# A metaformer block on one Trainium2 core: first x tile loaded by partition halves, W1's centring moved behind the router scores, first up-projection from copied weights

## The reference

```python
x = x + _L0_conv_ref(_ln_c(x), Wqkv, bqkv, Wout, bout, 8)       # _ln_c: norm over the 64 channels
t = _to_tokens(x)                                               # (8, 1024, 64)
t = t + _L0_ffn_ref(_ln_t(t), Wr, br, W1, b1, W2, b2, gamma, beta)
...
# attention:  qkv = Wqkv @ x + bqkv; attn = softmax(q k^T) per head, 8 x 8 over the channels;
#             out = Wout @ (attn @ v) + bout
# ffn:        logits = mean over tokens(x) @ Wr + br; softmax; capacity scale; softmax; top 2; softmax
#             h = gelu(x @ W1[e] + b1[e]);  y = h @ W2[e] + b2[e];  out = sum of w_e * y over the two experts
#             return layer_norm(out + x, gamma, beta)
```

## Time and profile before

| | |
|---|---|
| median of 3 runs | 97.44 us (97.40 to 97.64) |
| the profiled execution | 97.48 us |
| its span, first to last instruction | 95.7 us |
| mean granted clock of TensorE | 0.988 of full |
| busy: PE / DVE / ACT / POOL | 83.5 / 63.5 / 50.8 / 34.6 us |
| read from and written to HBM | 5.49 MB, 2.10 MB |

### The profile page before, as it was taken

How to read it: one execution, slowest core, us unless ns; L and a number is a source line. 1 busy time by engine, 2 the same in 40 slices (tenths; PEclk the granted TensorE clock), 3 DMA queues, 4 the chain that set the end, 5 groups by cost and what they waited for, 6 DMA issues and landing times.

```text
span 95.7 us, 2267 instructions
## 1 busy us (share of the span) xinstructions
PE 83.5 (87%) x765; PEld 45.0 (47%) x765; DVE 63.5 (66%) x223; ACT 50.8 (53%) x90; POOL 34.6 (36%) x83
## 2 busy tenths in 40 slices
PE   4993999999799999969749999999989999998800
PEld 1343696899664256649613327323333332335400
DVE  0089999992649799897998886326354464659350
ACT  0000474755487412406636999995997779643000
POOL 6000000003600000005434499949272660499900
PEclk9999999999999999999999999999999999999995
DMA  2899999950000000001430015686000026018654
GB/s 48 259 405 293 301 262 295 334 110 0 0 0 7 0 0 0 3 7 31 106 82 0 10 36 137 160 191 145 0 0 0 0 70 149 7 25 194 191 138 110
DMA packets 6554, 9.82 MB, mean 103 GB/s; under 512 B 1040, under 2 KB 3344, under 8 KB 6544
## 3 DMA queue, kind: packets, MB, share of 16 engines
q1 hardware_dynamic: 4688, 6.51, 26.2%
q10 hardware_dynamic: 1856, 3.18, 11.1%
HBM read 5.49 MB, written 2.10 MB: 79 GB/s over the span
## 4 chain that ended last, share of the span: by engine, by line
PE 43%; POOL 17%; DMA 10%; DVE 8%; ACT 7%; issue 6%; POOLq 4%; ACTq 1%; SPq 1%; DVEq 0%
DMA cst<-consts_dram 7%; POOL LO L518 7%; PE pB L970 4%; PE pS L970 4%; PE pA L980 4%; PE pC L1269 4%; POOL r L559 4%; ACT H L444 3%; POOLq L529 3%; POOL XT L248 3%; PE pA L1043 2%; PE pM L1057 2%; DMA ST<-LO 2%; PE pC L1031 2%; PE pS L1031 2%
## 5 line engine op out<-in xcount | busy, mean ns | idle before, releaser
L1269 PE MATMUL pC<-H,w2g 128*64 128x512 f32 x64 | 15.9, 603 | 0.0
L518 POOL TENSOR_TENSOR LO<-UF,HI 128x512 f16<-128x512 f32 x8 | 9.1, 1158 | 18.7 <-ACT HI L354 18.7
L652 DVE BATCH_NORM_STATS2 bst<-XT 128x6 f32<-128x128 f32 x32 | 6.5, 281 | 5.1 <-DMA XT<-x_tok_dram 5.1
L1161 PE MATMUL pM<-wz 128*128 128x512 bf16 x25 | 7.3, 456 | 1.3 <-POOL wz L511 1.3
L444 ACT ACTIVATE H<-pA,b1s 128x1024 f32<-128x1024 f32 x6 | 6.7, 1113 | 2.4 <-PE pA L1245 2.4
L534 POOL COPY w1g<-w1hl 128x256 f16 x14 | 5.2, 409 | 7.1 <-issue 5.0
L524 POOL TENSOR_TENSOR w1hl<-SQ,w1hl 128x512 f16<-128x512 f32 x2 | 2.3, 1159 | 15.0 <-DVE A L699 15.0
L361 ACT ACT_TABLE_LOAD x1 | 1.3, 1283 | 10.8 <-issue 10.8
L444 ACT ACTIVATE H<-pB,b1s 128x1024 f32<-128x1024 f32 x6 | 6.8, 1126 | 0.0
L354 ACT CAST HI<-UF 128x512 f16<-128x512 f32 x8 | 4.7, 617 | 3.3 <-DVE UF L758 3.3
L1269 PEld LDWEIGHTS pC<-H,w2g 128*64 128x64 f32 x64 | 3.9, 136 | 5.0 <-issue 4.0
(11 more groups left out here) (235 smaller groups left out, 190.8 us busy)
## 6 DMA issues: line engine op xcount, KB each, us to landing
out_dram<-XT SPq DMA_DIRECT2D x12, 128.0 KB, 2.4
XT<-x_tok_dram SPq DMA_DIRECT2D x2, 512.0 KB, 9.4
X<-x_cha_dram SPq DMA_DIRECT2D x8, 128.0 KB, 11.7
X<-x_cha_dram ACTq DMA_DIRECT2D x8, 128.0 KB, 11.5
ST<-HI SPq DMA_DIRECT2D x6, 128.0 KB, 2.4
ST<-LO SPq DMA_DIRECT2D x6, 128.0 KB, 2.4
XT<-x_tok_dram SPq DMA_DIRECT2D x2, 256.0 KB, 4.8
XT<-x_tok_dram ACTq DMA_DIRECT2D x2, 256.0 KB, 5.0
```

What stands on the lines that cost most here:

```text
L518: nc.gpsimd.tensor_tensor(LO[:, p, cols], UF[:, p, cols], HI[:, p, cols], ALU.subtract).then_inc(s["lo"], 1)
L652: return nc.vector.bn_stats(bst[:, p, j, :], XT[:, p, j * P:(j + 1) * P].rearrange("p (b c) -> p c b", b=2))
L1161: mm(pM[:, :], wz[:, 0:P], wz[:, :], start=True, stop=True)
L1269: last = mm(half(y_ps[:, b * HALF:(b + 1) * HALF], h), w2g[:, p % 2, b, k, :], H[:, step % 2, i, h * HALF:(h + 1) * HALF], start=False, st ...
```

## The change

- The first x tile `XT[0]` is loaded by partition halves: SP takes partitions 0 to 63 and ACT partitions 64 to 127, each in two column halves. All of X is loaded by SP.
- `scale1(1)` moves from DVE to POOL. The second warm-up has 2 matmuls for 5.
- `centre_w1` moves from behind `gram(1)` to behind the last `turn_scores`, with `split_w1` and `low_w1`; `centre_w2` moves behind the logits.
- The residual of pair 3, batch 0 is done by ACT (bias, into UF) and POOL (adding X) in DVE's place. The orders of `turn_t`, `scores` and `turned_stats` change, and `scores(3)` has a bank of its own.
- `spread2` of pairs 1 and 3 goes through `split3` on POOL, a new `turn2` on PE and a copy to `RR` on ACT, and then `spread`.
- `first_up` is gone: the first two units use `up`. ACT copies the weights of the first unit into `w1g`, POOL those of the others.
- `low(1, 1)` moves from POOL to DVE, in front of `evac_z(0)`.
- The last `scale_z` is two instructions of 256 columns, each waiting for its own part of `spread_last`.

On PE, behind `gram(1)` (the second block of L970 into pS), before: the two matmuls of W1's centring stand between the Gram matrix and `att_p1`.

The core of the diff:

```diff
-        ps_w1 = [pM[:, :], pB[:, HALF:N]]
+        ps_w1 = [pC[:, HALF:N], pA[:, 0:HALF]]
-        ps_st, ps_sc = pM, [pS, pB]
+        ps_st, ps_sc = [pM, pM, pM, pC], [pS, pB]
+        rb_last = [pA[:, HALF:HALF + HALF // 2], pM[:, 0:HALF // 2]]
...
-            for p in range(2):
-                sp.dma_start(XT[:, p, 0:HALF], x_tok[:, p, 0:HALF]).then_inc(s_xh[p][0], 16)
+            for h in range(2):
+                sp.dma_start(XT[0:C, 0, h * HALF:(h + 1) * HALF],
+                             x_tok[0:C, 0, h * HALF:(h + 1) * HALF]).then_inc(s_xh[0][h], 16)
+            sp.dma_start(XT[:, 1, 0:HALF], x_tok[:, 1, 0:HALF]).then_inc(s_xh[1][0], 16)
...
+                    for h in range(2):
+                        sp.dma_start(X[h * C:(h + 1) * C, p, b * HALF:(b + 1) * HALF],
+                                     x_cha[b * C:(b + 1) * C, p, h * HALF:(h + 1) * HALF]).then_inc(s_x[p], 16)
...
@@ ACT @@
+            act.wait_ge(s["conv"], 2 * NP - 1)
+            nc.scalar.activation(UF[:, NP - 1, 0:HALF], cv[NP - 1][0], ACT.Identity,
+                                 bias=cbs[:, B - 2:B - 1]).then_inc(s["cvb"], 1)
             evac_scores(1)
             square_means()
             evac_scores(2)
             evac_scores(3)
+            split_w1(0)
+            split_w1(1)
+            round_hi(0, 0)
+            act.wait_ge(s["rx1"], 1)
+            nc.scalar.activation(px[0], rout[:, 1, :], ACT.Exp).then_inc(s["rexp1"], 1)
+            act.wait_ge(s["rt2"], 1)
+            nc.scalar.copy(RR[:, :, :], ps_rt2.rearrange("p (k n) -> p k n", k=2)).then_inc(s["rr2"], 1)
+            round_hi(0, 1)
             act.wait_ge(s["w2p"], 1)
...
+            act.wait_ge(s["top"], 1)
+            first = {(0, 0): nc.scalar.value_load(i8[0:1, 0, 0:1], min_val=0, max_val=E - 1)}
+            nc.scalar.copy(w1g[:, 0, 0, 0, :, :], w1hl[:, bass.ds(first[0, 0], 1), :, :]).then_inc(s["w1g_first"], 1)
@@ POOL @@
+            pool.wait_ge(s_ut[0], 2)
+            scale1(nc.gpsimd, pool, 1)
...
+            nc.gpsimd.tensor_tensor(T[:, NP - 1, 0:HALF], UF[:, NP - 1, 0:HALF], X[:, NP - 1, 0:HALF],
+                                    ALU.add).then_inc(s["t3"], 1)
+            pool.wait_ge(s["pow2"], 1)
+            split3(nc.gpsimd, link, 0, 2, r2[:, 1:NP:2, :], s["s2"])
             low_w1(0)
             low_w1(1)
...
-            low(1, 1)
@@ DVE @@
+            dve.wait_ge(s["hi"], 4)
+            nc.vector.tensor_tensor(LO[:, 1, HALF:N], UF[:, 1, HALF:N], HI[:, 1, HALF:N],
+                                    ALU.subtract).then_inc(s["lo11"], 1)
...
-            scale_z(NP - 1, 1)
+            for i in range(2):
+                dve.wait_ge(s["rb3"], 2 * NP + i)
+                cols = slice(HALF + i * HALF // 2, HALF + (i + 1) * HALF // 2)
+                nc.vector.tensor_tensor(V[:, NP - 1, cols], ZS[:, NP - 1, cols], rb_last[i], ALU.mult).then_inc(s["vv"], 1)
@@ PE @@
-            warm_up(5)
+            warm_up(2)
             gram(0)
             transpose_u(0)
             gram(1)
-            centre_w1()
             att_p1(0)
...
+            turn_t(2, 0)
             scores(1)
-            turn_t(2, 0)
+            turn_t(2, 1)
             squares(1)
-            turn_t(2, 1)
+            turn_t(3, 0)
             turn_scores(0)
-            turn_t(3, 0)
+            turn_t(3, 1)
             turn_scores(1)
-            turn_t(3, 1)
             scores(2)
-            centre_w2(0)
+            scores(3)
             turn_scores(2)
-            scores(3)
-            centre_w2(1)
             turn_scores(3)
+            centre_w1()
             bias_logits()
             spread2(0, 0)
+            spread2(0, 1)
             logits()
-            spread2(0, 1)
+            turn2()
+            for i in range(2):
+                centre_w2(i)
+            for b in range(2):
+                spread2(1, b)
             for b in range(2):
                 spread2(2, b)
-            for b in range(2):
-                spread2(1, b)
```

More of the change, by code:

```diff
@@ L271, in _ @@
                 for half, src, done in ((0, HI, s["hi"]), (1, LO, s["lo"])):
-                    sp.wait_ge(done, 2 * p + 2)
+                    sp.wait_ge(done, 2 * p + 2 - half)
+                    if half:
+                        sp.wait_ge(s["lo11"], 1)
                     for h in range(2):
@@ L413, in first_expert @@
             def first_expert(k, b):
-                act.wait_ge(s["top"], 1)
-                return nc.scalar.value_load(i8[0:1, b, k:k + 1], min_val=0, max_val=E - 1)
+                if (k, b) not in first:
+                    first[k, b] = nc.scalar.value_load(i8[0:1, b, k:k + 1], min_val=0, max_val=E - 1)
+                return first[k, b]
             def square_last(b):
@@ L586, in _ @@
             experts = [[0, 0], [0, 0]]
-            for b in range(2):
-                experts[1][b] = load_expert(0, 1, b)
-                gather_w1(0, 1, b, experts[1][b])
-            for b in range(2):
-                experts[0][b] = load_expert(0, 0, b)
+            for k, b in ((0, 1), (1, 0), (1, 1)):
+                experts[k][b] = load_expert(0, k, b)
+                gather_w1(0, k, b, experts[k][b])
+            experts[0][0] = load_expert(0, 0, 0)
             pool.wait_ge(s["wkd"], 1)
@@ L1237, in up @@
             def up(step, i):
                 p, k, b = unit(step, i)
-                pe.wait_ge(s["w1g"], 2 * (TOP * p + k) + b - 1)
-                pe.wait_ge(s["gelu"], 2 * (step - 1) + i + 1)
+                if (step, b) == (0, 0):
+                    pe.wait_ge(s["w1g_first"], 1)
+                else:
+                    pe.wait_ge(s["w1g"], 2 * (TOP * p + k) + b)
+                if step >= 1:
+                    pe.wait_ge(s["gelu"], 2 * (step - 1) + i + 1)
                 for n, (a, src, done) in enumerate(((0, HI, s["hi"]), (1, HI, s["hi"]), (0, LO, s["lo"]))):
-                    if k == 0 and n != 1:
-                        pe.wait_ge(done, 2 * p + b + 1)
+                    if (k, p, b, n) == (0, 1, 1, 2):
+                        pe.wait_ge(s["lo11"], 1)
+                    elif k == 0 and n != 1:
+                        pe.wait_ge(done, 2 * p + b + 1 - (n == 2 and p >= 2))
```

124 lines of the change are left out of this document (66 added, 58 removed).

## The result

| | before | after |
|---|---|---|
| median of 4 runs of each | 97.54 us (97.40 to 97.87) | 99.77 us (98.67 to 100.17) |
| ratio, 95% interval | | 1.0175 [1.0124, 1.0225] |
| the profiled execution, span | 97.48, 95.7 us | 99.82, 97.7 us |
| mean granted clock of TensorE | 0.988 | 0.972 |

The forecast of 96.65 us and its range are missed on the slow side. The kernel before was timed again beside each group of kernels, and its median differs a little from place to place.

A forecast was written before the change was run, and what follows sets the result against it. By the chain of waits three places decide: the front on PE, the hand-over from routing to experts, the tail. 97.48 - 1.05 + 0 + 0.5 - 0.28 = 96.65 us, range 95.85 to 97.4.

The forecast's parts named there:

- Front: From the first loads to gram(2) on PE: gram(2) starts at 17.45 for 18.50, 1.05 us gained.
- alternative for `XT[3]`: In the front: if XT[3] lands 0.4 later for the extra issue, the gain at gram(2) is 0.75.
- X on SP: All of X's loads issued on SP behind XT[3]: costs nothing, hidden by the attention in between.
- Scores: From conv(3) to the last statistics and squares: DVE gives up one residual, PE is late; net 0, bounds -0.2 and +0.2.
- Routing to experts: Hand-over from router to expert units, up to up(4): first units' advance is lost at evac_z(0), 0.5 us lost.
- first-unit copies: First two expert units: pair 0's sums are done 0.75 to 0.9 ahead, a gain expected to be lost at evac_z(0).
- the upper bound: Routing to experts: low(1, 1) on DVE waits for POOL's four w2g and ends at 58.4; up to 1.6 lost.
- Tail: Last scale on DVE in two halves, one running while PE makes the rest: 0.28 us gained (0.2 to 0.3).
- Sum: Whole kernel: the terms added to the profiled time before give 96.65 us, held with 0.48.
- third rival: At evac_z(0): low(1, 1) on DVE is locked out by POOL's w2g, 1.6 later, total 97.75 us; chance 0.10.

The follow-up runs named there:

- e1_loads_back: Changed kernel with XT[0] loaded as before, by column halves of 128 partitions; 96.14 to 96.35 us in four of ten runs, ratio 0.9812 to before.
- e4_before_split: Kernel before with only XT[0] loaded by partition halves on both queues; 98.47 to 99.66 us in five of eleven runs, ratio 1.0103.
- e9_centre_back: e5_loads_dense with W1's centring back behind gram(1) and its splitting on ACT as before; 96.86 us, ratio 0.9934.
- e11_x_both_queues: e5_loads_dense with X loaded by SP and ACT as in the kernel before; 96.22, 96.33, 96.47 and 98.21 us, ratio 0.9873.
- e3_dense_spread3: Changed kernel with pair 3's spread again by 32 float32 matmuls instead of 8 bf16 ones; 98.88 us, ratio 1.0102.
- e10_first_up_back: e5_loads_dense with the first two units by first_up as in the kernel before; 95.93, 96.04, 96.26 and 97.49 us, ratio 0.9843.
- e8_tail_only: Kernel before with only the last scale in two parts of 256 columns, each waiting for its own eight matmuls; 97.35 us, ratio 0.9931.
- e5_loads_dense: Changed kernel with XT[0] loaded as before and pair 3's spread by 32 float32 matmuls as before; 96.11 us, ratio 0.9806.
- e12_longer_warm_up: e5_loads_dense with 25 matmuls in the first warm-up for 20; 95.79 to 96.34 us in four runs, 97.06 and 97.27 in two, ratio 0.9876.
- e7_order: e5_loads_dense with LO(1, 1) back on POOL and POOL's four w2g of pair 1 ahead of its two LO; 96.68 us, ratio 0.9859.
- e13_lo_behind: e5_loads_dense with LO(1, 1) and gc on DVE behind evac_z(0) instead of ahead of it; 97.33 us, ratio 0.9952.
- e15_full_halves: e5_loads_dense with XT[0] by partition halves, one DMA of 64 partitions by 1024 columns per queue; 98.16 us, ratio 0.9894.

## Why the prediction was wrong, by its own steps

- **Front, -1.05: measured +1.29; this is the step that failed.** The working took the gain from half the bytes and left "bounds 0, if the added issue delays XT[1], and 0.35". An issue was thus costed at nothing, and its downside at nothing too. It is 0.57 to 0.86 us on 64 partitions, for 0.38 to 0.44 on 128. The trace of before had this price: X's loads on 64 partitions stand there at 596 to 622 ns. Two of them ahead of everything moved the issue of `XT[1]` by 0.8 and that of the constants by 1.2. `XT[1]` landed 1.8 later, the constants 1.9, `XT[3]` 2.3, so about half of the delay is the issues' own time, and the rest is slower landing, for which no run gives the cause. e1_loads_back shows the whole edit as 2.1 us at gram(2), e4_before_split shows the same pattern in the old kernel (statistics end at 10.17 for 8.35). The prediction's alternative for `XT[3]`, 0.4 later, was right in kind and six times too small.
- The other steps of the front held. POOL scaled a half tile in 1.04, for the 1.27 taken, and gram(1) didn't wait. The centring gave 0.53 (e9_centre_back). With whole tiles gram(2) comes at 17.71 to 17.79, forecast 17.45: 0.7 to 0.8 of the 1.05.
- **X on SP, 0: right.** No residual waited. The Trainium skill ("DMA: Bandwidth & Descriptors", "Issuing engines are not separate DMA queues") says that issuing from several engines saves only the time it takes to initiate a DMA. The runs agree for X: on one queue or on two (e11_x_both_queues), no residual waited. That an issue's own time adds up on its queue the prediction said only for X, and it counted at `XT[0]`.
- **Scores, 0: measured -0.22** (from +1.29 to +1.07), at the end of its bounds.
- **Routing to experts, +0.5: measured +1.39** (from +1.07 to +2.46 at the last root, 90.12 for 87.66). The clock's fall is 1.35 of it by e3_dense_spread3 (1.37 by e1_loads_back); without it the term would be near 0. This is the second step that failed. The prediction had no term for pair 3's cheap spread, which takes work off PE, and named a falling clock only as what would make it wrong. Without the fall the stretch from wk on is little slower than before: 67.12 - 51.41 = 15.71 in e3_dense_spread3 and 65.87 - 50.65 = 15.22 before (from the second wk instruction to the Gelu behind up(4)), 0.5 more, the forecast's term. Only, wk itself came 0.45 ahead (from +1.07 to +0.62), where the forecast had 0.07, so the two nearly cancel.
- **Inside it:** first-unit copies win 0.9 at the second Gelu and nearly nothing at the end (e10_first_up_back), as forecast. The order "DVE subtraction, then evac_z" came as forecast, at 0.68. What the upper bound feared for LO(1, 1), a wait for POOL's w2g, didn't come: w2g got longer instead (1.57 for 1.04), and it was `hb` that waited, for POOL's LO. The Trainium skill ("SBUF — State Buffer", "SBUF: two separate sides") says that a DVE instruction with two SBUF inputs and one of POOL that reads SBUF exclude each other for a whole instruction. The runs agree: one `hb` takes 0.23 or 0.31 where no LO of POOL has started ahead of it, and 1.09 where one has.
- **Tail, -0.28: measured -0.33** in the trace (from +2.46 to +2.13), and -0.48 in the medians of e8_tail_only, above its upper bound of 0.3.
- **Sum.** 97.48 + 1.29 - 0.22 + 1.39 - 0.33 = 99.61; the profiled execution took 99.82, and 0.21 lies behind the last add and around the span. The third rival had the right sign by the wrong mechanism; no rival held the price of an issue. Three slips in the working change nothing: its terms for gram(2) add to 17.49 for the 17.45 written, 46.3 with 0.9 and 0.4 is 47.6 for 47.8 (measured 48.68 - 1.07 = 47.6), and the third rival's 58.4 less 56.88 is 1.5 for 1.6.

Still open: why the loads behind the two halves land more slowly than their issues explain, and why PE's clock falls in some executions of one kernel and not in others. e1_loads_back in its profiled execution had PE busy 0.83 of 2 us and then 1.04 of 2 at 56 to 60 us and kept 1.00, the changed kernel fell after 0.92 and 0.95. Slower runs are still there with the idle time filled in one place, one of six in e5_loads_dense and two of six in e12_longer_warm_up; that they became rarer isn't shown.

## What to carry to other kernels

Price every DMA issue at the head of a queue by a row of the same partition count, and move everything behind it by at least that; here splitting the first load so that it landed 0.7 us earlier delayed all others, the second by 1.8 and the fourth by 2.3. Before work is taken off TensorE, look at what is left around it, and give a falling clock a price and a chance: taking off 32 matmuls cost nothing in an execution that kept the clock and 1.35 us in one that didn't. Among operations with two SBUF inputs on DVE and POOL, moving one to the other engine changed who waited here and brought no time.

## What the runs showed of the hardware

- An issue of a DMA on 64 partitions took its queue 571 to 862 ns (512 columns) and 577 to 591 (1024 columns), one on 128 partitions by 512 columns 382 to 444 ns where the queue had only such ahead of it, but 589 to 616 behind two of 64, and 560 to 844 behind one. On 64 partitions the length didn't matter (571 and 577 ns for the first on SP), and the queue's past did. The partition count alone doesn't give the time: `XT[2]` and `XT[3]`, 128 partitions by 1024 columns, took 431 to 887 ns.
- PE at half clock: gram(0)'s 16 matmuls took 2.03 us at 1.00 and 3.4 to 3.5 where the clock fell (e7_order, e13_lo_behind, e15_full_halves), behind 1.86 us of PE's waiting for the constants in e7_order and 2.04 in e15_full_halves; but e5_loads_dense waited 2.03 and kept 1.00.
- In e9_centre_back the fall came 4 us behind the emptiest stretch, with PE busy 1.8 and 1.98 of 2 in between.
- A product of 128 x 64 on DVE took 0.23 to 1.10 us by what ran on POOL, one of 128 x 1 0.16 or 0.77.
